# Queries, keys and weights transposed by DMA, and one accumulator for four groups of heads

## The reference

```
x = x + global_latent_attn(rmsnorm(x, norm1_w), ...)   # causal over all 2048 tokens
x = x + local_gqa_attn(rmsnorm(x, norm2_w), ...)       # causal, the last 32 tokens only
# in both:
q = split_heads(x @ wq, H)
q, k = (rope(q, base), rope(k, base))
q, k = (qk_norm(q), qk_norm(k))
scores = einsum('bhqd,bhkd->bhqk', q, k) / sqrt(HD)
out = merge_heads(softmax(where(mask, scores, -1e30)) @ v) @ wo
```

## Time and profile before

| | |
|---|---|
| median of 3 runs | 556.69 us (556.41 to 556.72) |
| profiled execution | 556.19 us, of which the span of the core 554.5 |
| mean granted clock of TensorE | 0.947 of full speed |
| PE, matrix products | 457.3 us busy (82%), 6400 instructions |
| DVE | 373.9 us (67%), 1010 |
| ACT | 355.8 us (64%), 490 |
| POOL | 194.8 us (35%), 480 |

### The profile page before, as it was taken

One profiled execution on the slowest core, in us unless ns is written; L12 is line 12 of the kernel. 1 busy time (PEld: TensorE's weight loads), 2 busy tenths in 40 slices (PEclk: granted clock), 3 DMA queues, 4 the chain that ended last, 5 costly groups with the idle time before them and its releaser, 6 DMA issues.

```text
span 554.5 us, 16532 instructions
## 1 busy us (share of the span) xinstructions
PE 457.3 (82%) x6400; PEld 248.8 (45%) x6400; DVE 373.9 (67%) x1010; ACT 355.8 (64%) x490; POOL 194.8 (35%) x480
## 2 busy tenths in 40 slices
PE   0258778999999989999999999899998997548263
PEld 0124334545464445644654554454545544424241
DVE  2889987675756866788588658667146566765456
ACT  0033857688977979688689878976897986104010
POOL 3555647676601465331056202601043011041101
PEclk9999979899999999999999999999999999858676
DMA  8300000000000000000000000000000000000000
GB/s 203 96 1 1 2 3 1 1 4 3 1 2 3 11 2 4 2 1 13 2 6 8 3 1 12 1 2 11 3 2 2 3 7 6 1 0 12 0 1 9
DMA packets 8811, 6.25 MB, mean 11 GB/s; under 512 B 1816, under 2 KB 8096, under 8 KB 8736
## 3 DMA queue, kind: packets, MB, share of 16 engines
q1 hardware_dynamic: 5312, 2.52, 1.8%
q10 hardware_dynamic: 3424, 2.68, 1.7%
HBM read 4.15 MB, written 1.05 MB: 9 GB/s over the span
## 4 chain that ended last, share of the span: by engine, by line
PE 47%; DVE 31%; POOL 9%; issue 8%; ACT 4%; SPq 1%; DVEq 1%; DMA 1%; POOLq 0%; ACTq 0%
PE osum_g L980 14%; PE scores L953 9%; PE scores L947 4%; PE misc L1088 4%; PE misc L1077 4%; PE misc L980 3%; ACT prob L801 3%; DVE early L1206 2%; PE misc L997 2%; DVE qe_g L1313 2%; DVE early L1478 1%; DVE early L1439 1%; PE misc L907 1%; DVE early L1202 1%; POOL prob L743 1%
## 5 line engine op out<-in xcount | busy, mean ns | idle before, releaser
L801 ACT ACTIVATE prob<-scores 128x1024 f32<-128x1024 f32 (+3 forms) x352 | 308.2, 929 | 100.0 <-PE scores L953 96.9
L980 PE MATMUL osum_g<-prob,V 128*32 128x256 f32 (+1 forms) x2304 | 148.7, 381 | 4.5 <-POOL prob L743 2.9
L953 PE MATMUL scores<-qT,kT 32*128 32x256 f16 (+3 forms) x1520 | 106.6, 257 | 15.6 <-ACT prob L801 11.0
L980 PEld LDWEIGHTS osum_g<-prob,V 128*32 128x32 f32 x2304 | 63.4, 111 | 57.7 <-issue 29.1
L743 POOL TENSOR_SCALAR_AFFINE_SELECT prob<-prob 128x512 f32<-128x512 f32 x64 | 43.2, 690 | 104.7 <-ACT prob L801 104.3
L953 PEld LDWEIGHTS scores<-qT,kT 32*128 32x128 f16 x1520 | 35.8, 92 | 90.5 <-issue 84.0
L760 POOL TENSOR_SCALAR frs<-fmv 128x1 f32<-128x1 f32 x16 | 3.1, 195 | 115.0 <-DVE fmv L1494 114.7
L1088 PE MATMUL misc<-t2T,h1p 128*128 128x512 f16 x128 | 34.6, 419 | 9.1 <-DVE h1p L1471 9.1
L1077 PE MATMUL misc<-early,t1T 128*128 128x256 f16 x256 | 33.6, 291 | 1.4 <-DVEq L1442 1.3
L1478 DVE TENSOR_TENSOR early<-misc,oh 128x512 f32<-128x512 f32 x32 | 22.0, 686 | 15.9 <-PE misc L1088 14.8
L947 PE MATMUL scores<-band,identb 128*32 128x320 bf16 (+1 forms) x512 | 27.4, 305 | 3.0 <-DVEq L1338 2.1
(11 more groups left out here) (228 smaller groups left out, 724.8 us busy)
## 6 DMA issues: line engine op xcount, KB each, us to landing
X<-in_L_attn_hidden_dram SPq DMA_DIRECT2D x8, 128.0 KB, 4.8
early<-in_L_ffn_expert_w_dram ACTq DMA_DIRECT2D x1, 1024.0 KB, 7.9
out_dram<-X SPq DMA_DIRECT2D x16, 64.0 KB, 1.5
rope<-in_rope_dram SPq DMA_DIRECT2D x1, 256.0 KB, 3.7
early<-in_L_ffn_shared_w_dram ACTq DMA_DIRECT2D x2, 128.0 KB, 8.9
band<-in_band_dram ACTq DMA_DIRECT2D x1, 80.0 KB, 3.1
wraw_l<-in_L_attn_l_wq_dram ACTq DMA_DIRECT2D x1, 64.0 KB, 2.7
ident<-in_ident_dram SPq DMA_DIRECT2D x1, 64.0 KB, 2.5
```

The costliest lines, as they stand in the source:

```text
L801: act.activation(prob[:, n % NP, 2 * half:2 * half + 2, lo:hi], src, ACT.Exp, scale=float(HD) ** -0.5 * QSCALE ** -2).then_inc(exp_done, 1)
L953: ins = pe.matmul(scores[:, 512 * m + c:512 * m + c + w], kT[a][rows, g, P * (t % kept[a]):P * (t % kept[a]) + P], qT[a][rows, b % Q_KEPT[ ...
L980: ins = pe.matmul(o[32 * m:32 * m + 32, q:q + w], V[a][:, t % kept[a], g, :], prob[:, n % NP, m, c:c + w], start=(first and k == 0), stop= ...
```

## The change

- `kT`, `qT` and `wturn` are no longer steps of PE and DVE. SP issues a DMA transpose from SBUF to SBUF instead: one for the keys (128 x 8 x 128 two-byte elements), one for the global queries, two of half the size for the local ones, and two for all the weights (128 x 18 x 128 each). SP gets a list of its own from the planner, with the output stores in it. The layouts of `kT`, `qT` and `t2T` change to what the DMA writes.
- The four groups of a block and layer share one accumulator bank. V's window for a group is still 32 columns wide, but one half of it is zeros: groups 0 and 1 add into the two halves of the same 32 partitions, groups 2 and 3 do the same 256 columns further (`V_AT`, `at`). There is one copy (128x512) and one `oT` step with four transposes, one reciprocal and one product. `wo`'s rows are put in the matching order before launch.
- `NP` is 4 instead of 3. The planner has a fifth engine, and a table of 14 x 8 offsets (`PULL`) in the place of `KNOBS`' factors, so all lists are new.

```diff
-NP = 3
+NP = 4
+V_AT = [0, 32, 96, 128]
-PE, DVE, POOL, ACT_E = range(4)
-HOP = (0.22, 0.1, 0.08, 0.2)
+PE, DVE, POOL, ACT_E, SP = range(5)
+HOP = (0.22, 0.1, 0.08, 0.2, 2.5)
...
+PULL = {
+    "unitg": (749.2, 939.7, 409.5, 154.3, 1050, 121.7, 460.4, 510.3),
...
-        op((PE, "kT", a, b), 0.55, (POOL, "ksplit", a, b), bank=[((DVE, "kT", a, b), 0)])
-        op((DVE, "kT", a, b), 0.69, (PE, "kT", a, b), *([("Q", L, p, KVH - 1, 0)] if b > 1 and not g else []))
-        op((PE, "qT", a, b), 0.55, (DVE, "split", a, b), bank=[((DVE, "qT", a, b), 0)])
+        op((SP, "kT", a, b), 0.5, (POOL, "ksplit", a, b), *([("Q", L, p, KVH - 1, 0)] if b > 1 and not g else []))
         o = b - Q_KEPT[a]
-        op((DVE, "qT", a, b), 0.69, (PE, "qT", a, b), *([("Q", a, o, *units_of(a, o)[-1])] if o >= 0 else []))
+        op((SP, "qT", a, b), 0.5, (DVE, "split", a, b), *([("Q", a, o, *units_of(a, o)[-1])] if o >= 0 else []))
...
-        qT = [sb(f"qT{a}", [P, Q_KEPT[a], KVH, QB], F16) for a in (G, L)]
+        qT = [sb("qT0", [P, Q_KEPT[G], 2, KVH, P], F16), sb("qT1", [P, Q_KEPT[L], KVH, QB], F16)]
-        kT = [sb(f"kT{a}", [P, KVH, kept[a] * P], F16) for a in (G, L)]
-        V = [sb(f"V{a}", [P, kept[a], KVH, 32]) for a in (G, L)]
+        kT = [sb(f"kT{a}", [P, kept[a], KVH, P], F16) for a in (G, L)]
+        V = [sb(f"V{a}", [P, kept[a], VW]) for a in (G, L)]
...
+            def w_turn(k):
+                sp.wait_ge(tern_ready, 5 if k else 3)
+                o, t = (t2T[:].rearrange("p e f d -> p (e f) d"), t2) if k else (t1T[:], t1)
+                sp.dma_start_transpose(o, t).then_inc(wt_in, 16)
+            def k_turn(a, b):
+                sp.wait_ge(kpart_ready[a], b + 1)
+                old = b - kept[a] // 2 + 1
+                if a == L and old >= 1:
+                    sp.wait_ge(qk_done, 2 * UNIT[(L, old, KVH - 1, 0)] + 2)
+                t = 2 * b % kept[a]
+                sp.dma_start_transpose(kT[a][:, t:t + 2].rearrange("p t g k -> p (t g) k"),
+                                       ke[a][:].rearrange("p i g r t d -> p (i g r t d)")).then_inc(kT_in[a], 16)
+            def q_turn(a, b):
+                sp.wait_ge(part_ready[a], b + 1)
+                old = b - Q_KEPT[a]
+                if old >= 0:
+                    sp.wait_ge(qk_done, 2 * UNIT[(a, old, *units_of(a, old)[-1])] + 2)
+                o = qT[a][:, b % Q_KEPT[a]]
+                if a == G:
+                    sp.dma_start_transpose(o.rearrange("p i g q -> p (i g) q"),
+                                           qe[a][:].rearrange("p i h t d -> p (i h t d)")).then_inc(qT_in[a], 16)
+                else:
+                    for i in range(2):
+                        sp.dma_start_transpose(o[:, :, P * i:P * i + P],
+                                               qe[a][:, i].rearrange("p h t d -> p (h t d)")).then_inc(qT_in[a], 16)
...
-            def o_copy(a, b, g):
-                act.wait_ge(pv_done, PV[ENDS[(a, b, g)][1]] + 1)
+            def o_copy(a, b):
+                act.wait_ge(pv_done, PV[ENDS[(a, b)][1]] + 1)
...
-                act.copy(oTs[a][:, g, :], o[:, 0:QB]).then_inc(f, 1)
+                act.copy(oTs[a][:].rearrange("p r q -> p (r q)"), o[:]).then_inc(f, 1)
...
             def pv_product(*u):
-                first, last = [u == x for x in ENDS[(a, b, g)]]
+                first, last = [u == x for x in ENDS[(a, b)]]
...
-                    s = ("pv", L, b, g, 0)
-                    take(pe, s)
+                    s = ("pv", L, b, 0, 0)
+                    if g == 0:
+                        take(pe, s)
...
+                at = QB * (g // 2)
...
-                        ins = pe.matmul(o[32 * m:32 * m + 32, q:q + w], V[a][:, t % kept[a], g, :],
+                        ins = pe.matmul(o[32 * m:32 * m + 32, at + q:at + q + w], V[a][:, t % kept[a], V_AT[g]:V_AT[g] + 32],
...
-                for g in range(KVH):
-                    ins = pe.transpose(bank(s)[:, P * g:P * g + P], oTs[a][:, g, P * i:P * i + P], ident[:])
+                for i in range(2):
+                    for r in range(2):
+                        ins = pe.transpose(bank(s)[:, P * (2 * i + r):P * (2 * i + r) + P], oTs[a][:, r, P * i:P * i + P], ident[:])
```

More of the change, by code:

```diff
@@ L302, in make_plan @@
     ready, ended = dict(steps.earliest), {}
-    waiting, order, free = [[], [], [], []], [[], [], [], []], [0.0] * 4
+    waiting, order, free = [[] for _ in range(5)], [[] for _ in range(5)], [0.0] * 4 + [9.0]
     queues = [[("Q", a, b, *u) for b in range(NB) for u in units_of(a, b)] for a in (G, L)]
@@ L343, in make_plan @@
         options = [[(t, urgent[k], k) for k in waiting[PE] if (t := bank_wait(k)) is not None],
-                   *[[(ready[k], urgent[k], k) for k in waiting[e]] for e in (DVE, POOL, ACT_E)]]
+                   *[[(ready[k], urgent[k], k) for k in waiting[e]] for e in (DVE, POOL, ACT_E, SP)]]
         n = len(units)
@@ L358, in make_plan @@
         best = None
-        for e in range(4):
+        for e in range(5):
             if options[e]:
```

277 lines of the change are left out of this document (112 added, 165 removed).

## The result

The changed kernel takes 529.11 us, median of four runs (525.26 to 532.36), beside 556.55 us for the kernel before on the same chip (556.37 to 556.72). The ratio is 0.9504, 95% interval 0.9439 to 0.9569: 27.4 us less. The forecast was 525.0 us with a range of 511 to 543. The profiled execution took 528.51 us.

The account below looks back on a forecast made before the run. PE was taken to bound the middle; 26.7 + 1.2 + 0.3 + 3.0 + 0.5 = 31.7 us less than 556.19 gave 524.5, so 525.0 us as median, with a range of 511 to 543.

Parts of the forecast that it names:

- What bounds the kernel: Between 60 and 460 us PE is busy 377.98 of 400 us, so work taken from it should save time nearly one for one.
- Transposes off PE and half the output turns, 26.7 us: Middle stretch: 18.12 us of key, query and weight transposes leave PE, plus 8.59 us from halving the output transposes.
- my terms: Summed savings counted for the parts: 18.12 and 8.59 us in the middle, 1.2 at the start, 0.3, 3.0 and 0.5 at the end.
- Idle time kept at 22 us: Middle stretch: PE's idle time was left at 22 us, with bounds from no gain to 26.7 + 10 us.
- the rival of the half-hidden gain: Middle: where ACT is full, freed PE time becomes waits for exponentials, 9.3 us lost, 534.3 us; chance 0.20.
- A DMA transpose takes 3.7 us: Keys and queries: 3.7 us from ready data to landing, ends 1.5 and 8.9; SP takes 0.44 us per issue.
- the 3 to 5 us that I named as a sign of being right: Sign for the forecast: each DMA transpose lands within 3 to 5 us of its issue.
- The start, 1.2 us: First block: queries land by DMA at 33.9 us, against first scores at 35.10 before, so 1.2 us earlier.
- The last global PV product, near 435 us: Sign for the forecast: the last global PV product ends near 435 us instead of 466.
- the list of signs: What would show the forecast right or wrong: PE's busy share, last global PV product, transpose landings, end length, waits, first scores.
- The end, 3.8 us: Last local block: scores 0.3 us earlier, 3.0 from the moved feed-forward product, 0.5 from the shorter close.
- The wait that was named as a sign against: Sign that the forecast is wrong: scores that wait for a transpose in the middle.

Follow-up runs that it names:

- run 12: Work of the kernel before (neither part), with four probability buffers and a finer table fitted to it: 556.85 us, ratio 0.9998 to the kernel before.
- run 9: The changed kernel with three buffers of probabilities in place of four and a table fitted for three: 540.38 us, ratio 0.9697 to the kernel before.
- Run 7: The changed kernel in its own order, with a local block's queries turned by one DMA of eight blocks: 523.22 us, again 523.77.
- run 2: The changed kernel with one more DMA transpose into an unused tile ahead of each block's key and query transposes, same order: 555.13 us, ratio 0.9958.
- run 3: The changed kernel with one planner number, `whole`, back at 0.25 instead of 0.02, everything planned anew, table not refitted: 553.64 us, ratio 0.9935.
- runs 4, 5: The changed kernel with one part only, four buffers, each with a fitted table: accumulator alone (4) 544.45 us, DMA transposes alone (5) 547.58 us.

## Why the prediction came out right, by its steps

**What bounds the kernel.** Right. PE is busy for 95% of the middle (364.7 of 382.4), the last global PV product ends at 442.5 (near 435 was forecast, 466.0 before), and the gain is in the middle by five sixths.

**Transposes off PE and half the output turns, 26.7 us.** The mechanism was right and the size too large. The work went as counted, but the middle shrank by 23.6 us with the start's gain in it, where my terms made 27.9. I took PE's other work as constant. It is not, for the order decides how many score units are split, and a split one costs PE up to twice. Against the kernel before that returned 4.1 us in score products, and 8.7 of busy time came back in all. Against run 12, whose order was made in the same way, the middle shrank by 26.4 us, so the terms fit the work better than they fit the comparison with the old order. The shares of the parts failed most: for the transposes 19.6 us were counted, and alone they gave 11; for the accumulator 9.1, and alone it gave 13.

**Idle time kept at 22 us.** Nearly right as a number (23.0 became 17.7) and wrong as a reason. With three buffers it is 28.5 (run 9) and the time 540 us: there part of the freed time turned into waits for exponentials and masks, as the rival of the half-hidden gain has it. The fourth buffer, which I had priced at nothing in the forecast and named only among the rivals, kept 11 us of idle time away. Two errors of opposite sign covered each other: waits that freed time turns into, and a buffer that had no price. That the sum came out within 4.1 us is in part luck.

**A DMA transpose takes 3.7 us.** The medians are 2.4 us for four blocks and 2.7 to 2.8 for eight, faster than taken and below the 3 to 5 us that I named as a sign of being right; single ones took up to 4.9. All are inside my bounds of 1.5 and 8.9. I missed SP: an issue takes 1.24 us, not the 0.44 of the earlier trace rows, which is the issue of a plain DMA. Three in a row put the local queries' scores 4.8 us behind their readiness at the end of the run (474.42 - 469.61), where my 0.44 gave 4.1. The Trainium skill, page "VectorE: DVE Perf Modes", section "The three transpose paths", has a figure for one block by which eight would take 10.5 us, the estimate of the prediction. The trace has 2.7 to 2.8, so figures of single blocks do not add up.

**The start, 1.2 us.** It is 2.15 us: 32.95 in place of 35.10, since the DMA landed 0.9 us sooner than taken.

**The last global PV product, near 435 us.** It ends at 442.5. The forecast's own terms put it at 466.0 - 26.7 - 1.2 = 438.1, so 3 of the 7 us are a slip of the list of signs.

**The end, 3.8 us.** The stretch behind the last global PV product is 84.3 us in place of 88.5, so 4.2. From the first scores of the last local block to the end of the span it is 52.3 us (526.7 - 474.42) in place of 55.6 (554.5 - 498.90), 3.3 of the 3.5 forecast for the product that no longer stands between local units and for the shorter close. The 0.3 us forecast for the scores' earlier start did not come: before as after they start 4.8 us behind the queries' readiness. As run 12 shows, a fitted order gives 2.6 us of the end without either part.

**The wait that was named as a sign against.** "Scores that wait for a transpose in the middle" did appear, 6.4 us in three places. It was not enough to turn the result. Run 7 shows what it costs, about 5 us, and run 2 what one extra transpose on SP ahead of each costs: the whole gain, about half of it through the waits and half through the clock.

**Open.** Why the two parts together give 5 us more than their sum is not settled: each kernel has its own order, and an order by itself moved the time by up to 26 us (run 3). The fits of runs 4, 5, 9 and 12 were made in the same way, but I can't show that each is equally close to its best. Why some transposes land after 4 to 5 us is open too, and so is what decides whether a gap of 2.5 to 3 us on PE is followed by the lower clock.

## What to carry to other kernels

When work is taken from the engine that bounds a kernel, ask first whether its neighbours have a buffer to keep up: here about 11 of the 28 us came only with one more buffer, which was worth nothing before. Count a DMA queue's issue time like an engine's: here a transpose held the issuing queue for 1.24 us, with four blocks as with eight, so one of eight was better than two of four. And where an order was fitted to a kernel, no single edit is measured fairly until the order is fitted again, and the fair base is the old work with an order fitted in the same way.

## What the runs showed of the hardware that was not expected

A transpose of two-byte data from one tile of the chip's memory to another by DMA lands 2.4 us after its issue for four blocks of 128x128 and 2.7 to 2.8 for eight, as the median; single ones in the changed kernel took up to 4.5 and 4.9. SyncE is held for about 1.25 us in both cases (longest 1.85). For the 18 blocks of the weights it lands after 4.5 to 4.6, and SyncE is held for 2.7.

Score products of 32 rows for four heads, in the four quarters of TensorE's rows, take the same time as those for two heads: 0.40 us for eight beside 0.39 for four, and 0.33 for twelve narrow ones beside 0.32 for six.

A gap of PE in a full stretch can be paid again: with 13.2 us more of idle time (run 2) the same products took 14.3 us longer, and ten slices have a granted clock of 0.66 to 0.92. It need not be: one wait of 2.92 us left the clock at full and one of 2.59 us in the same execution did not. The changed kernel's own four runs spread by 1.3% (525.26 to 532.36) beside 0.1% for the kernel before. Of the four the slowest has the lowest clock of the record (0.932, against 0.950 for the fastest). Over more runs the kernel before spreads too, by 0.8% (554.52 to 558.96).
